# A fused six-stage decoder kernel: stage 5 begun inside stage 4's end, late chunks summed in two banks, and a reordered opening

## What is computed

```
x = ln(x + ssm_mixer(x))                 # stage 0
x = ln(x + cross_attention(x, ctx, mask))# stage 1, 16 heads
x = ln(x + moe(x))                       # stage 2, 16 experts, top 4
x = ln(x + windowed_attention(x))        # stage 3, 8 heads
x = ln(x + causal_cross_attention(x, concat(ctx, x)))   # stage 4, 16 heads
x = ln(x + moe_with_capacity(x) + shared(x))            # stage 5
```

```
delta = softplus(dt + delta_param); a_bar = exp(-delta * abs(dt))
x = silu(conv(z_x)); h = a_bar * h + x (outer) B; y = h . C
y = rmsnorm(sigmoid(u @ W_gate) * y) * norm_w;  return y @ W_out
```

## Time and profile before

| what | value |
|---|---|
| runs, us | 737.38, 737.55, 740.12; median 737.55 |
| profiled execution | 736.69 us, span 734.9 us |
| TensorE (PE) busy | 681.5 us, 93% of the span |
| VectorE (DVE), ScalarE (ACT), GpSimd (POOL) busy | 455.7, 386.7, 82.5 us |
| mean granted TensorE clock | 0.992 |

### The profile page before, as it was taken

One profiled execution on the slowest core, in us unless ns is written; L12 is line 12 of the kernel. 1 busy time (PEld: TensorE's weight loads), 2 busy tenths in 40 slices (PEclk: granted clock), 3 DMA queues, 4 the chain that ended last, 5 costly groups with the idle time before them and its releaser, 6 DMA issues.

```text
span 734.9 us, 20035 instructions
## 1 busy us (share of the span) xinstructions
PE 681.5 (93%) x8426; PEld 351.8 (48%) x8428; DVE 455.7 (62%) x1133; ACT 386.7 (53%) x725; POOL 82.5 (11%) x83
## 2 busy tenths in 40 slices
PE   6899999989899888999998899999998899999897
PEld 3354545455555543444444445556555344443342
DVE  0684545555678957668587655656663667628753
ACT  2747474746777663424442236565553535554556
POOL 1382222230000000000002012111110000000000
PEclk9999999999999999999999999999999999999999
DMA  8400000000000013541500000000000000016430
GB/s 344 208 4 1 4 0 4 0 4 2 1 3 1 2 46 72 117 95 28 110 3 3 3 0 4 3 3 4 3 4 3 0 1 0 0 36 219 134 106 29
DMA packets 11784, 29.49 MB, mean 40 GB/s; under 512 B 1128, under 2 KB 1512, under 8 KB 11176
## 3 DMA queue, kind: packets, MB, share of 16 engines
q1 hardware_dynamic: 11696, 28.22, 13.0%
HBM read 26.97 MB, written 1.25 MB: 38 GB/s over the span
## 4 chain that ended last, share of the span: by engine, by line
PE 68%; DVE 12%; ACT 9%; issue 6%; DMA 3%; POOL 0%; SPq 0%; DVEq 0%; ACTq 0%
PE banks L1834 5%; PE banks L2454 4%; PE banks L2395 4%; PE banks L2078 3%; PE banks L2090 3%; PE banks L2445 3%; PE banks L2405 3%; PE banks L2083 3%; PE banks L2230 3%; DVE sb_rowmax L1181 2%; PE banks L2167 2%; PE banks L2291 2%; PE banks L1870 2%; PE banks L1887 2%; PE banks L2295 2%
## 5 line engine op out<-in xcount | busy, mean ns | idle before, releaser
L1834 PE MATMUL banks<-sb_xT,sb_arena 128*128 128x512 f32 x128 | 59.1, 610 | 6.6 <-DMA sb_arena<-w 6.6
L912 ACT ACTIVATE sb_arena<-banks 128x512 f32<-128x512 f32 x64 | 34.8, 607 | 52.2 <-PE banks L2261 52.2
L1516 DVE TENSOR_REDUCE sb_rowmax<-banks 128x4 f32<-128x512 f32 x64 | 41.2, 686 | 28.4 <-PE banks L2252 28.4
L819 ACT ACTIVATE sb_arena<-banks 128x512 f32<-128x512 f32 x36 | 21.5, 597 | 51.1 <-PE banks L2078 51.0
L646 ACT ACTIVATE sb_arena<-banks 128x512 f32<-128x512 f32 x64 | 35.0, 599 | 24.7 <-PE banks L1834 24.6
L1104 DVE TENSOR_TENSOR sb_arena<-banks,sb_arena 128x512 f32<-128x512 f32 x32 | 21.0, 686 | 34.7 <-PE banks L1887 34.6
L1834 PEld LDWEIGHTS banks<-sb_xT,sb_arena 128*128 128x128 f32 x128 | 24.5, 195 | 36.3 <-issue 32.5
L572 POOL TENSOR_TENSOR sb_arena<-sb_la,sb_consts 128x1024 f32<-128x1024 f32 x16 | 33.1, 2081 | 73.8 <-PE banks L1870 54.2
L1739 DVE TENSOR_TENSOR sb_arena<-sb_arena,sb_w 128x512 f32<-128x512 f32 x32 | 21.2, 686 | 30.4 <-ACT sb_arena L982 29.0
L2090 PE MATMUL banks<-sb_arena,sb_w 128*128 128x512 f32 x72 | 36.1, 601 | 2.2 <-DVE sb_arena L1399 2.2
L2230 PE MATMUL banks<-sb_arena 32*64 32x512 f32 x256 | 35.4, 612 | 2.5 <-ACT sb_arena L912 1.4
(11 more groups left out here) (334 smaller groups left out, 1468.2 us busy)
## 6 DMA issues: line engine op xcount, KB each, us to landing
sb_arena<-weights_by_expert SPq DMA_DIRECT2D x16, 512.0 KB, 8.0
sb_w<-weights_by_expert SPq DMA_DIRECT2D x32, 256.0 KB, 3.6
sb_w<-w SPq DMA_DIRECT2D x1, 2646.5 KB, 21.9
sb_w<-w SPq DMA_DIRECT2D x1, 1736.0 KB
sb_consts<-consts SPq DMA_DIRECT2D x1, 1227.0 KB, 10.4
sb_arena<-w SPq DMA_DIRECT2D x2, 512.0 KB, 5.7
sb_ctxT<-ctx SPq DMA_DIRECT2D x1, 1024.0 KB, 12.2
sb_xT<-x SPq DMA_DIRECT2D x1, 768.0 KB, 8.1
```

The lines of the kernel that those rows point to most:

```text
L912: act.activation(probT4[k % 2][:, g].rearrange("p b j q -> p (b j q)"), by_key[g][:], ACT.Exp).then_inc(s_e4, 1)
L1516: dve.tensor_reduce(rowmax4[k % 2][:, 4 * g:4 * g + 4], bank[n][:].rearrange("p (j t) -> p j t", j=4), AX, ALU.max).then_inc(s_mx4, 1)
L1834: pe.matmul(bank[(4, 5, 0, 1)[n % 4]][:], bc_w_tiles[:, n, :], cols(c), start=True, stop=True).then_inc(s_v, 1)
```

## The change

Opening: w0 is loaded right after x's first columns; TensorE first takes three products of zeros (a tile that VectorE sets), then waits for x and w0, does the branch's projection first, and then the B and C tiles. ScalarE copies the branch first, takes the branch's tanhs after tile 12 and the gate's after tile 15. VectorE no longer waits for the constants, starts the taps at once, and does the dt steps (`dt_summed`, `decays_of_dt`) between and after them.

Stage 0 to 1: the three operands are made in stage 0's last chunk before the gating, the table load moves to that chunk too, and ScalarE's k copies no longer wait for the memset.

Stage 4 to 5: chunk 0's four tiles up are placed around pv4(15); ScalarE takes their GELUs before chunk 3's norm, with a table load more; the norm's products come after tiles 5 and 7, and chunk 1's first tile up before the router product. The counts begin after n = 5 of chunk 2, so two fewer lie in the shared branch and two more in the experts; the rank products come one expert later. shared_plus_x moves forward in VectorE's order.

Late chunks: chunk 2 is summed in bank 3 and chunk 3 in bank 4, the wait for s_resid is gone, and the bias product follows the ninth down tile (BIAS_AT = 8).

```diff
--- before.py
+++ after.py
@@ -216,6 +216,7 @@
     decay = [take(NH * SEQ).rearrange("p (h t) -> p h t", h=NH) for _ in range(2)]
+    zeros = decay[1][:, 0:8, :].rearrange("p h t -> p (h t)")
@@ -458,9 +459,10 @@
+    late_sum, BIAS_AT = (bank[3], bank[4]), 8
     SEARCH_FROM = 2
-    COUNT_AT = (0, 2, 4, 6)
-    RANKS_AT = (11, 12, 13)
+    COUNT_AT = {2: (5, 7), 3: (1, 3, 5, 7)}
+    RANKS_AT = (12, 13, 14)
@@ -499,10 +501,10 @@
         sync.dma_start(xT[:, 0:CHUNK], dram["x"][:, 0:CHUNK]).then_inc(s_x0, 16)
+        sync.dma_start(w_sb[0][:], dram["w0"][:, skip0:]).then_inc(s_w[0], 16)
...
             sync.dma_start(bc_w[:, a:a + n], dram["w0"][:, a:a + n]).then_inc(loaded, 16)
-        sync.dma_start(w_sb[0][:], dram["w0"][:, skip0:]).then_inc(s_w[0], 16)
@@ -655,11 +657,12 @@
-            def tanhs():
+            def x_tanhs():
...
                     act.activation(th[:, m], xh[:, m], ACT.Tanh).then_inc(s_th, 1)
+            def gate_tanhs():
@@ -667,18 +670,21 @@
+            if is_first(c):
+                x_copies(0)
...
                         dt_steps()
-                    if n == 7:
-                        x_copies(0)
+                    if n == 12:
+                        x_tanhs()
                     if n == 15:
-                        tanhs()
+                        gate_tanhs()
...
                     if n == 7:
-                        tanhs()
+                        x_tanhs()
+                        gate_tanhs()
@@ -696,7 +702,9 @@
                 act.activation(Ls[u % 2].rearrange("p h t -> p (h t)"), bank[2 + u % 2][:], ACT.Exp).then_inc(s_L, 1)
-            if not is_last(c):
+            if is_last(c):
+                load_set(act, EXP_LN_SET)
+            else:
@@ -737,11 +745,10 @@
             if is_first(c):
-                load_set(act, EXP_LN_SET)
...
                 act.wait_ge(s_y, TILES * NCH)
+                pre1(0, 0)
                 act.wait_ge(s_z1, 1)
-                pre1(0, 0)
@@ -953,19 +960,21 @@
             if c == 0:
-                for part in range(4):
-                    hook(part)
...
                 act.activation(act5[n], bank[n][:], ACT.Gelu, bias=w(5, "sb1")[:, n:n + 1]).then_inc(s_sge, 1)
-                if c == 0 and n == 0:
-                    wait(act, s_zt, NCH)
-                    act.wait_ge(s_pv4, 4 * NCH)
-                    act.wait_ge(s_t4, 16 * NCH)
-                    act.wait_ge(s_po4, NCH)
-                    act.activation(sg5, zt, ACT.Tanh, scale=0.5).then_inc(s_th5, 1)
+            if c == 0:
+                load_set(act, EXP_LN_SET)
+                for part in range(4):
+                    hook(part)
+                load_set(act, GELU_SET)
+                wait(act, s_zt, NCH)
+                act.wait_ge(s_pv4, 4 * NCH)
+                act.wait_ge(s_t4, 16 * NCH)
+                act.wait_ge(s_po4, NCH)
+                act.activation(sg5, zt, ACT.Tanh, scale=0.5).then_inc(s_th5, 1)
@@ -1002,7 +1011,7 @@
                     out_ahead5(q - 1)
-                if q == RANKS_AT[2] + 1:
+                if q == RANKS_AT[2]:
@@ -1035,22 +1044,26 @@
         def setup_dve():
+            dve.memset(zeros, 0.0).then_inc(s_prep, 1)
...
                 dve.memset(spare[:, n:n + 1], 0.0).then_inc(ahead, 1)
-            dve.wait_ge(s_const, 16)
...
             dve.tensor_scalar(cw[:, 0:8], w(0, "conv_w"), 0.5, None, ALU.mult)
-            dve.tensor_scalar(cw[:, 8:10], w(0, "conv_b"), 0.5, None, ALU.mult)
+            dve.tensor_scalar(cw[:, 8:10], w(0, "conv_b"), 0.5, None, ALU.mult).then_inc(s_prep, 1)
+            dve.wait_ge(s_prep, 2)
+
+        def dt_summed():
...
             last.then_inc(s_prep, 1)
-            dve.wait_ge(s_prep, 1)
...
             dve.tensor_tensor(dtz[:], dt, w(0, "delta").unsqueeze(1).to_broadcast([P, NH, NH]), ALU.add).then_inc(s_dtc, 1)
+
+        def decays_of_dt():
@@ -1059,7 +1072,8 @@
         def front0(c, hook, nxt):
-            settled(dve)
+            if not is_first(c):
+                settled(dve)
@@ -1073,6 +1087,10 @@
                                              op0=ALU.mult, op1=ALU.add).then_inc(s_cv, 1)
+                if is_first(c) and i == 5:
+                    dt_summed()
+            if is_first(c):
+                decays_of_dt()
@@ -1116,6 +1134,11 @@
                     dve.tensor_copy(bcol[:, n + 1:n + 2], b).then_inc(s_bcol, 1)
+            if is_last(c):
+                dve.wait_ge(s_w[1], 16)
+                dve.tensor_tensor(qb[:], const("group"), w(1, "bq").to_broadcast([P, 2]), ALU.mult).then_inc(s_p1, 1)
+                dve.tensor_tensor(kb[:], const("inner"), w(1, "bk").to_broadcast([P, 4]), ALU.mult).then_inc(s_p1, 1)
+                dve.tensor_scalar(mneg[:], w(1, "mask"), -1000000000.0, None, ALU.mult).then_inc(s_p1, 1)
@@ -1150,12 +1173,7 @@
             if is_first(c):
-                dve.wait_ge(s_w[1], 16)
                 dve.wait_ge(s_ctx, 16)
-                dve.wait_ge(s_bcp, 1)
-                dve.tensor_tensor(qb[:], const("group"), w(1, "bq").to_broadcast([P, 2]), ALU.mult).then_inc(s_p1, 1)
-                dve.tensor_tensor(kb[:], const("inner"), w(1, "bk").to_broadcast([P, 4]), ALU.mult).then_inc(s_p1, 1)
-                dve.tensor_scalar(mneg[:], w(1, "mask"), -1000000000.0, None, ALU.mult).then_inc(s_p1, 1)
@@ -1634,7 +1652,6 @@
                 step(dve.max(m85[:, k, :], sg5[:, k, :]), more=(k < 15))
-            shared_plus_x(0)
@@ -1649,6 +1666,7 @@
             step(dve.tensor_reduce(tm5, wt5, AX, ALU.add))
+            shared_plus_x(1)
@@ -1733,7 +1751,7 @@
                 if i >= 4:
-                    wait(dve, s_f2, 17 * n + i - 2)
+                    wait(dve, s_f2, 17 * n + i - 3 + (i - 4 > BIAS_AT))
@@ -1751,14 +1769,14 @@
             hook(1)
+            shared_plus_x(0)
...
             weights5()
-            shared_plus_x(1)
...
                 search(it)
-                if it == 5:
+                if it == 2:
                     shared_plus_x(2)
-                if it == 9:
+                if it == 7:
@@ -1770,7 +1788,7 @@
             for h in range(2):
-                dve.tensor_tensor(half_tokens(resid, h), bank[3][:, h * HALF:(h + 1) * HALF],
+                dve.tensor_tensor(half_tokens(resid, h), late_sum[1][:, h * HALF:(h + 1) * HALF],
@@ -1788,7 +1806,7 @@
                     wait(dve, s_f2, 17 * (c - AHEAD) + 17)
-                    dve.tensor_tensor(resid[:], bank[3][:], total, ALU.add).then_inc(s_resid, 1)
+                    dve.tensor_tensor(resid[:], late_sum[c - AHEAD][:], total, ALU.add).then_inc(s_resid, 1)
@@ -1799,11 +1817,14 @@
         def setup_pe():
+            pe.wait_ge(s_prep, 1)
+            for _ in range(3):
+                pe.matmul(bank[6][:], zeros[:, 0:P], zeros, start=True, stop=True)
             pe.wait_ge(s_x0, 16)
+            pe.wait_ge(s_w[0], 16)
...
             pe.wait_ge(s_x_in, 16)
-            pe.wait_ge(s_w[0], 16)
@@ -1820,6 +1841,8 @@
+            if is_first(c):
+                x_projected(0)
@@ -1832,8 +1855,6 @@
                 pe.matmul(bank[(4, 5, 0, 1)[n % 4]][:], bc_w_tiles[:, n, :], cols(c), start=True, stop=True).then_inc(s_v, 1)
-                if is_first(c) and n == 5:
-                    x_projected(0)
@@ -1841,7 +1862,7 @@
                 pe.wait_ge(s_const, 16)
-                pe.wait_ge(s_prep, 1)
+                pe.wait_ge(s_prep, 3)
@@ -2323,7 +2344,14 @@
                         wait(pe, s_vx4, 4 * (i // 2))
+                    if i == PAIRS + 1:
+                        pe.wait_ge(s_mx4, 16 * NCH)
+                        shared_up5(0, 0)
+                        shared_up5(0, 1)
                     pv4(i - 2)
+                    if i == PAIRS + 1:
+                        shared_up5(0, 2)
+                        shared_up5(0, 3)
@@ -2372,20 +2400,26 @@
+        def shared_up5(c, n):
+            wait(pe, s_sge, 4 * c + n - 3)
+            pe.matmul(bank[n][:], s1v[:, n, :], cols(c), start=True, stop=True).then_inc(s_sf1, 1)
+
         def shared5(c, hook, it):
-            for n in range(8):
+            for n in range((4, 1, 0, 0)[c], 8):
                 if n < 4:
-                    wait(pe, s_sge, 4 * c + n - 3)
-                    pe.matmul(bank[n][:], s1v[:, n, :], cols(c), start=True, stop=True).then_inc(s_sf1, 1)
+                    shared_up5(c, n)
...
                     pe.matmul(bank[4][:], s2v[:, n - 4, :], act5[n - 4], start=(n == 4), stop=(n == 7)).then_inc(s_sf2, 1)
-                if c == 0 and n < 3:
-                    hook(n + 1)
-                if c >= SEARCH_FROM and n in COUNT_AT:
-                    count(it + COUNT_AT.index(n))
+                if c == 0 and n == 5:
+                    hook(2)
+                if c == 0 and n == 7:
+                    shared_up5(1, 0)
+                    hook(3)
+                if c >= SEARCH_FROM and n in COUNT_AT[c]:
+                    count(it + COUNT_AT[c].index(n))
@@ -2447,11 +2481,11 @@
             pe.wait_ge(s_fold, FOLD)
```

(15 more changed lines are left out.)

## The result

The changed kernel took 719.84 us in the median of 4 runs (718.37 to 720.58), beside 738.84 of four runs of the kernel before made with them (737.38, 737.55, 740.12, 745.93): ratio 0.971, 95% interval 0.966 to 0.976. Its profiled execution took 720.57 with a span of 718.8; before's had 736.69 and 734.9. The direction and the places were right. Ratios and intervals are taken over the fast runs and the medians over all, so a ratio is not the quotient of the medians beside it.

A forecast was written before the change was run, and what follows sets the result against it. TensorE, busy 93% of the span, bounds the kernel, so only its idle, slow or late places pay: 4.1 + 3.2 + 4.2 + 0.7 + 3.0 = 15.2 off 736.69 gives 721.5, median 722.3; range 717.5 to 729.

The forecast's parts named there:

- The median of the runs is 0.86 higher: 722.3.: Last step of the sum: from a profiled execution of 721.5 to the median of the runs, 722.3.
- Opening, 4.1: Start to the first chunk's recurrence: earlier full-speed tiles, copies and tanhs bring it 4.1 us earlier; bounds 2.4 and 4.9.
- So 22.8: Opening: TensorE starts at 6.3 and, at full speed, reaches the end of tile 12 at 22.8 us.
- the upper bound: Opening: 4.9, if the level is full from the first zeros and part of three copies hides beside gate tiles.
- The first rival, zeros that do not raise the clock in time: Opening: up to four records cost 0.43 more each, 1.7 in all, giving 724.0; chance 0.12.
- Stage 0 to 1, 3.2: Stage 0 to 1: k copies start right behind ScalarE's squares, table already loaded, 3.2 us earlier; bounds 2.0 and 3.3.
- Stage 4 to the late chunks, 4.2: Stage 4's end through the search: TensorE's idle pieces and waits, 4.8, less 0.6 left, 4.2 earlier; bounds 2.5 and 4.8.
- The third rival, later counts that give it back: Search: it runs behind, TensorE waits in the experts or for ranks; 4.2 shrinks to 1, giving 725.5; chance 0.08.
- Late chunks, 0.7 + 3.0: Late chunks: chunk 2's bias product no longer waits, 0.7; chunk 3's bank wait goes, 4.0 - 1.0 = 3.0.
- The second rival: Chunk 3: its wait only moves to VectorE, tiles 1 to 3 stall, one of 3.0 left, 724.3; chance 0.10.
- the main case: Chunk 3: Ln follows the table load at once, down 4 begins 4.0 earlier behind GELU 4; 3.0 kept after the bias product.
- The stages in between have no wait on absolute time, so what is won should stay won: Stages between the four changed places: once the weights have landed, gains at one place should be kept.

The follow-up runs named there:

- with fill: Kernel before plus 30 products that nobody reads where TensorE waits, 20 around stage 1's first k and v products, 10 at chunk 3's sum: 736.24 us, ratio 0.995.
- the three edits of the kernel before: Kernel before with dt products in three groups (ratio 0.996), with 30 products that nobody reads (0.995), and with both of these (0.993).
- the kernel before with both edits: Kernel before with the dt products in three groups and the 30 products that nobody reads: 734.07 us, ratio 0.993.

## Why the prediction was off, point by point

**The failed step is the last one of the sum: "The median of the runs is 0.86 higher: 722.3."** The forecast set the changed kernel's median 0.86 above its profile; it came out equal to it (720.56 and 720.57), while before's median lies 4.3 above its own. The sum was made against one profiled execution, and the clock's low stretches were counted only where that execution had them, at 163 and 699. (It had a third, 0.63 from 420 to 424, in code that the change leaves alone; all fourteen traces have one somewhere from 392 to 424.) The runs showed that the kernel before has others in many executions. Four places tell it, by the windows of fourteen traces:

| place | code | traces with low clock |
|---|---|---|
| behind the dt products, 15 to 22 us | in one block, before's opening | 2 of 5 |
| same | in one block, the changed opening | 4 of 5 |
| same | in three groups, either opening | 0 of 4 |
| stage 0 to 1, 156 to 168 us | as before | 2 of 5 |
| same | with fill, or changed | 0 of 9 |
| stage 4 to 5, around pv4(15) and the first tiles up | TensorE idle three times | 5 of 7 |
| same | tiles up around pv4(15) | 1 of 7 |
| chunk 3's first down tile | waits for the bank, as before | 5 of 5 |
| same | with fill, or in the second bank | 0 of 9 |

In before's own trace the first and the third place read 1.00; of the seven traces with its order at stage 4 to 5, only one other does there. The windows of the kernel with stage 0 to 1 alone changed show what it looks like:

```profile
564.00:568.00 4.00, 2.57 (x73) 2.15 (x62) 1.25 (x2) 0.00 (x0) 0.00 (x0) 0.53 0.02 4
568.00:572.00 4.00, 4.00 (x6) 1.72 (x7) 1.83 (x9) 0.63 (x1) 0.00 (x0) 0.62 0.00 0
```

Behind the dt products the change does not remove the fall, which comes at least as often with the changed opening; it makes it cheap. The first chunk begins at 34.67 to 35.34 in the three traces of before's opening without the fall and at 38.86 and 40.56 in the two with it; in the changed opening with its zeros it begins at 30.44 in the trace without the fall and at 31.40 to 31.45 in the three with it. The averages are 36.9 and 31.2, a gain of 5.7, where before's own trace, the earliest of its five, gives 3.2 to 4.2. So part of the surplus is that before's profiled execution had a lucky opening.

That the low clock costs time, and not only goes with it, is supported by the three edits of the kernel before, which keep its schedule and take away such occasions (the dt block, stage 0 to 1, chunk 3's start): by the ratios they gave 3.0, 3.9 and 5.1, by the medians 4.5, 4.6 and 6.8, and no interval holds zero. How much of that is the clock stays open: for the last, the mean clock explains 2.7, and the interval begins at 2.9. Nor is it shown that the clock makes the whole surplus of the change. Stage 4 to 5 alone left the mean clock of its runs where it was (0.9882, beside 0.9879 for before), although five traces of seven show the fall there before and one of seven after, and its gain is no more than its profile shows.

**Opening, 4.1: the term of the sum that was mis-sized.** Its edits alone gave 8.4 (interval 5.9 to 11.0), about twice the term. In profiles of the changed opening it is 4.2 without the fall behind the dt products and 3.2 to 3.3 with it, so against before's own trace the term held. What it left out is how often before's opening is later than in that trace: by the averages above that brings it to 5.7, and the other 2.7 stay open. The steps were right one by one: TensorE began at 6.25 (forecast 6.3) at full speed, the taps were done early, the table load stood before the copy of tile 13. "So 22.8" for tile 12 missed the low clock behind the dt products, which moved the table load to 25.29. With the products in three groups it was 4.6 and 4.8, near the upper bound. The Trainium skill (SBUF — State Buffer, Who interferes with whom) was borne out on the moved taps: 1.22 without GpSimd beside them, 4.12 with it.

**The first rival, zeros that do not raise the clock in time**, fell: 4 records behind them took 1.96 (1.88 to 2.16 in all six traces with zeros), and without them 3.75. In one of the six the zeros ran past w0's arrival at 6.13, and the branch began at 6.73. The clock did vary, but later, behind the dt products. The Trainium skill (TensorE: Matmul & The Clock Gate, Part 1: The HAM clock gate) says that the number of slow matmuls at a start differs between runs of one kernel; the traces here agree: the first eight records of before's opening took 5.30 in its own trace, 5.70 and 5.87 in two others with the same start. Far from the start the same instructions ran at 0.50 and at 1.00, too (16 to 20 us).

**Stage 0 to 1, 3.2:** measured 3.3, by the mechanism given; the clock is full there.

**Stage 4 to the late chunks, 4.2:** measured 4.6 from the router product of chunk 2 to the first late tile. The third rival, later counts that give it back, fell with two waits of 0.3 in all.

**Late chunks, 0.7 + 3.0:** measured 3.0. Chunk 2 gave 0.3 and chunk 3 2.7. The second rival happened only as far as forecast in the main case: Ln's wait went and down 4 is the next thing late: it begins 1.5 after the tile before it, which takes 0.9, and its row shows 0.49 idle. Between tiles 1 and 2 the variance product waits 0.4 for ScalarE's square; otherwise tiles 1 to 3 don't stall.

**"The stages in between have no wait on absolute time, so what is won should stay won":** true in sign, but not exact. From the first scores to the router product of chunk 2 the changed kernel gained 2.8 in code that is the same. In the stretch of stages 3 and 4 between the same two products (430.19 and 550.03 in before) the thirteen other traces need 115.4 to 120.2, before's 119.8, after's 116.8, and the clock doesn't separate them: it reads 1.00 throughout. Of the 4.4 us between before's trace and the shortest one (the kernel before with both edits), TensorE's busy time holds 2.2 (114.70 and 112.51), idle pieces that the profile calls issue 1.6, and waits for other engines 0.4; the cause stays open. By this before's profile is one of the longest here (second of fourteen) while its clock was among the best. So 16.1 against 15.2 is partly two errors that cancel: opening and late chunks 2.4 smaller than summed (2.4 + 3.0 against 4.1 + 3.7), the unchanged stages 2.8 larger.

## What to carry to other kernels

Don't add a saving worked out on one execution to a median: list each place where TensorE idles or runs narrow products for several microseconds. At each of them the low clock may or may not have come in the trace at hand, so count its price with a chance, and profile the kernel before more than once. In this kernel such places were mended for little, by spreading narrow products between wide ones or with products that nobody reads (3.0 to 5.1 by the ratios), without reordering anything else. When a change moves the median more than the profiles, compare the granted clock of all the runs first.

## What the runs showed of the hardware

- A low clock can follow a solid block of narrow products although TensorE is busy throughout: behind 32 records of 16 columns in 3.6 us, 6 traces of 10 read 0.51 to 0.77 from 15 to 22 us, and the others 1.00. Split into three groups between 512-column products, none of 4 did. That the block is the cause is likely by these counts and by the gain of splitting it in the kernel before (interval 0.5 to 5.3), and not proven.
- A low clock at the same place can have very different prices: behind the changed opening's dt products (0.76 to 0.77 from 15 to 22 us) the first chunk began 1.0 later (31.4 against 30.44), behind before's (0.51 and 0.57) 3.5 to 5.9 later.
- The mean granted clock of one kernel's 68 executions ranges from 0.979 to 0.997, and its time from 733.0 to 748.7 with it (correlation 0.86).
- The same instructions of stages 3 and 4 took between 115.4 and 120.2 us in fourteen traces, at a clock of 1.00, for a cause that stays open.
